# A gated linear-attention recurrence on one Trainium2 core: small products as tiles of TensorE, and a new order of the pieces

## The chip, the cores and the metric

One core of one Trainium2 chip runs the whole program. The metric is the device time of one execution in microseconds (us); less is better. TensorE (PE) multiplies, VectorE (DVE), ScalarE (ACT) and GpSimd (POOL) do elementwise work, SyncE (SP) issues most transfers. Before the change the median of 3 runs is 4453.52 us (4452.66 to 4456.73).

## The reference, cut to what matters

The program computes two layers over 16 x 1024 tokens of 256 features: a normalization, a recurrent attention block, a mixture of 8 experts (expert choice), a second recurrence (a linear state-space scan) and a gated feed-forward block. The change touches the recurrent attention block alone:

```python
delta = shifted - h
x_lerp = h + delta * x_proj_mu
x0 = jnp.tanh(x_lerp @ xl_w1.T) @ xl_w2.T + xl_b2          # 256 -> 32 -> 160
x1 = jnp.tanh(x0).reshape(B_, T_, 5, R)                    # 5 groups of 32
x2 = jnp.einsum('btnr,hnr->btnh', x1, x_out_w.reshape(H_, 5, R))
mus = x2 + x_bias
r_mu, w_mu, k_mu, v_mu, g_mu = (mus[:, :, i] for i in range(5))
r = (h + delta * r_mu) @ r_w.T
w_in = h + delta * w_mu
w = jnp.tanh(w_in @ w_w1.T) @ w_w2.T + w_b                 # 256 -> 64 -> 128
k = (h + delta * k_mu) @ k_w.T
v = (h + delta * v_mu) @ v_w.T
g = (h + delta * g_mu) @ g_w.T
wd = jnp.exp(-jnp.exp(w.reshape(B_, T_, NH, DK)))
...
o_t = jnp.einsum('bhk,bhkv->bhv', r_t, S) + jnp.sum(r_t * bonus * k_t, -1, keepdims=True) * v_t
S = S * w_t[..., None] + k_t[..., None] * v_t[..., None, :]
...
o = (o * gn_weight + gn_bias) * jax.nn.silu(g)
return o @ o_w.T
```

There are 4 heads of 32 keys and 64 values. All of it is fp32.

## The kernel before, in words

The function `recurrence_phase` cuts the 1024 tokens of each of the 16 sequences into chunks of 128. A **group** is 4 sequences times one chunk of 128 tokens, so 512 tokens (`GN`); there are 32 groups (`GROUPS`), in order. Tiles hold features on the 128 partitions and the 512 tokens along the free dimension.

Three sorts of work are interleaved, in an order written out by hand in `sequence`, which every engine walks through:

- `piece(f, ...)`: the projections of group f, from the mixed input to receptance, keys, decay, values and gates. Each product has a number `n`, `bank(n)` says in which PSUM bank it lands, `emptied` waits until ACT or DVE has read an earlier product. The products by name: LOW (256 -> 32, tile a_low), X0 and X0T (32 -> 128 and 32 -> 32, tiles a_x1 and a_x1t), ten mixing products MIX (a_xo and, for the fifth mixture, a_xot; two for each of five mixtures), DLOW (256 -> 64) and DEXP (64 -> 128) for the decay, KEY, REC, OWN (the token's own product r*bonus*k, summed by heads, 4 columns at a time), two of VAL and two of GATES. After a mixing product DVE forms a_tmp (L1164), then POOL a_mix (L1077).
- `level(g, lv)`: seven levels that build the 128 x 128 lower triangle A of products inside a chunk. In each, PE multiplies keys by receptance for 4 sequences x 4 heads as row tiles of 32 (L1467) into the four banks `ps_heads` (banks 0 to 3, the level banks); then DVE scales keys, receptance and decay (L1190, L1192, L1194) and, in levels 0 to 4, copies the products under a mask into a_A (L1203); in levels 5 and 6 ACT copies them (L1322). PE begins the next level when both are done. At level 0 the copy also waits until ACT has written the diagonal of A: 16 activations (L1299, tile a_A) that follow ACT's copy of OWN (L1295, a_own).
- `chunk(g, u)`: transposed keys (L1481), the outputs o from the state and from A (L1501, L1504; two halves), the update U of the state (L1493), the normalization (reduction L1231, `pow` on POOL L1091, scaling L1236), transposes (L1516), gating (L1241) and the output product with a_ow.

Before the change all pieces use banks 6 and 7 in turn, and all but the levels and U are products on the whole array; where the weight has only 32 or 64 rows it is padded with zero rows to 128. While group g goes through its levels, the pieces of group g+1 and the rest of the chunk of g-1 fill the spaces. POOL's `ahead` computes a_delta for group g+2, and DVE's `begin` computes a_lerp (L1148) for it. A matmul in fp32 appears in the profile as two instructions (two passes).

Of the kernel before, what the change touches and what calls it, by code (L numbers as in the profile page):

```python
# [735 lines left out]
def recurrence_phase(nc, ctx, ps, ps_heads, xnT_d, s0_d, acc_d, left_d, ident, score, idxT, gateT, idxL, gateL, w):  # L736

    with ExitStack() as mem:
# [11 lines left out]
        w2 = sb("a_w2", [P, NMU * RANK])  # L750
        b2 = sb("a_b2", [P, 1])
        b2t = sb("a_b2t", [RANK, 1])
        xo = sb("a_xo", [P, NMU - 1, D])
        xot = sb("a_xot", [P, D])
# [6 lines left out]
        dw2 = sb("a_dw2", [P, KW])  # L761
# [10 lines left out]
        low = sb("a_low", [P, GN])  # L772
        x1 = sb("a_x1", [P, GN])
        x1t = sb("a_x1t", [P, GN])
        tmp = [sb(f"a_tmp{r}", [P, GN]) for r in range(2)]
        mix = [sb(f"a_mix{n}", [P, KD, GN]) for n in range(NMU)]
        dlow = sb("a_dlow", [P, GN])
# [91 lines left out]
        LOADS = 21  # L869
        PADDED = 7  # L870
        SET = PADDED + 8
        READY = SET + NH + 2
        order = [1, 2, 0, 3, 4]
        SLOTS = 9
        CHUNK = LEVELS
        LATE = 2
        FRONT = SLOTS - LATE + 1
        MIX = [3, 4, 5, 6, 8, 9, 13, 14, 16, 17]
        LOW, X0, X0T, DLOW, DEXP, KEY, REC, OWN, VAL, GATES = 0, 1, 2, 7, 10, 11, 12, 15, 18, 20
        USES = 22  # L880
        BY_ACT = [LOW, X0, X0T, DLOW, DEXP, KEY, REC, OWN, VAL, VAL + 1]
        BY_DVE = MIX + [GATES, GATES + 1]
        AT = {2: (0, 1), 3: (2, 3), 4: (4, 5), 6: (6, 7), 7: (8, 9)}
# [6 lines left out]
        def later(j, q, n):  # L890

            return (j + (q + n) // QB, (q + n) % QB)

        def emptied(eng, f, n):

            if n < 0:
                f, n = f - 1, n + USES
            if n in BY_ACT:
                eng.wait_ge(act_out, len(BY_ACT) * f + BY_ACT.index(n) + 1)
            else:  # L900
                eng.wait_ge(dve_out, len(BY_DVE) * f + BY_DVE.index(n) + 1)

        def bank(n):
            return ps[6 + n % 2]

        def sequence(eng, ahead, begin, piece, level, chunk, extra=None):

            def group(j, q, first, left):
                g = QB * j + q
                f1, f2 = later(j, q, 1), later(j, q, 2)  # L910
                r = q % 2

                def chunk_at(s):
                    if s >= CHUNK:
                        chunk(g, j, q, s - CHUNK, first)
                    elif not first:
                        jp, qp = later(j - 1, q, QB - 1)
                        chunk(g - 1, jp, qp, s + SLOTS - CHUNK, isinstance(j, int) and j == 0 and q == 1)

                def piece_at(s):  # L920
                    if s < LATE:
                        piece(g, q, FRONT + s, first)
                    elif left:
                        piece(g + 1, f1[1], s - LATE if s < CHUNK else s - LATE + 1, False)

                for s in range(SLOTS):
                    if s < LEVELS:
                        level(g, r, s, first)
                    if left and s == CHUNK:
                        piece(g + 1, f1[1], CHUNK - LATE, False)  # L930
                    if extra and s == CHUNK:
                        extra(g, s)
                    if s < LATE or s == SLOTS - 1:
                        piece_at(s)
                        chunk_at(s)
                    else:
                        chunk_at(s)
                        piece_at(s)
                        if extra and s < CHUNK:
                            extra(g, s)  # L940
                    if left > 1 and s == CHUNK:
                        ahead(g + 2, f2[0], f2[1])
                    if left > 1 and s == SLOTS - 1:
                        begin(g + 2, f2[1], False)

            ahead(0, 0, 0)
            begin(0, 0, True)
            for s in range(FRONT):
                piece(0, 0, s, True)
            ahead(1, 0, 1)  # L950
            begin(1, 1, False)
            for q in range(QB):
                group(0, q, q == 0, 9)
            for j in range(1, NE - 1):
                for q in range(QB):
                    group(j, q, False, 9)
            for q in range(QB):
                group(NE - 1, q, False, QB - 1 - q)
            for u in range(SLOTS - CHUNK, SLOTS):
                chunk(GROUPS - 1, NE - 1, QB - 1, u, False)  # L960
# [4 lines left out]
        def _(sp):  # L965
            loads = [(mu[:], w["L0_attn_x_proj_mu"]), (w1[:], w["L0_attn_xl_w1"]),
                     (b2[:], w["L0_attn_xl_b2"][0:P]), (b2t[:], w["L0_attn_xl_b2"][P:P + RANK]),
# [5 lines left out]
            for dst, src in loads:  # L973
                sp.dma_start(dst, src).then_inc(w_in, 16)
            padded = [(w2[0:RANK, :], w["L0_attn_xl_w2"]), (dw2[0:GATE, :], w["L0_attn_w_w2"]),
                      (xot[0:RANK, :], w["L0_attn_x_out_w"][P:P + RANK])]
# [5 lines left out]
            assert len(loads) + len(padded) == LOADS + 1  # L982

            def load(j, q, first):
                for k in range(KD):
                    if first:
                        sp.dma_start(h[q % 2][:, k, :, 1:P + 1], hT_v[k, :, GT * q:GT * (q + 1), 0:P]
                                     ).then_inc(h_in[q % 2], 16)
                    else:
                        sp.dma_start(h[q % 2][:, k], hT_v[k, :, GT * q:GT * (q + 1), bass.ds(P * j - 1, P + 1)]  # L990
                                     ).then_inc(h_in[q % 2], 16)

            def store(j, q):
                sp.wait_ge(s0_sb, 2 * (QB * j + q) + 2)
                sp.sem_inc(spare, 1)
                sp.dma_start(s0_v[bass.ds(j, 1), :, GT * q:GT * (q + 1), :].rearrange("o p b d -> (o p) b d"),
                             s0[q % 2][:]).then_inc(s0_out[q % 2], 16)

            def group(j, q, first):

                f2 = later(j, q, 2)
                sp.wait_ge(mixed, NMM * (QB * j + q + 1))
                sp.sem_inc(spare, 1)
                load(f2[0], f2[1], first and q < 2)
                if not first or q:
                    store(*((j, q - 1) if q else (j - 1, QB - 1)))

            load(0, 0, True)
            load(0, 1, True)
            for q in range(QB):  # L1010
                group(0, q, True)
            for j in range(1, NE - 1):
                for q in range(QB):
                    group(j, q, False)
            for q in range(QB):
                if q < 2:
                    group(NE - 1, q, False)
                else:
                    store(NE - 1, q - 1)
# [7 lines left out]
            store(NE - 1, QB - 1)  # L1027
# [5 lines left out]
        def _(pool):  # L1033
            nc.gpsimd.memset(zeros[:], 0.0).then_inc(zeroed, 1)
            for operand in (xo, w2, xot, dw2, low, x1t, dlow):
                nc.gpsimd.memset(operand[:], 0.0).then_inc(set_up, 1)
# [15 lines left out]
            pool.wait_ge(w_in, 16 * (LOADS + 1))  # L1052
# [13 lines left out]
            def begin(f, q, first):  # L1066
                pass
# [13 lines left out]
            def level(g, r, lv, first):  # L1081
                pass
# [1205 lines left out]
```

## Time and profile before

| | us |
|---|---|
| median of 3 runs | 4453.52 |
| the profiled execution, its own time | 4459.22 |
| its span | 4456.3 |
| the recurrence, from its first to its last product (213.2 to 1759.8) | 1547 |
| one group of it, in the middle (716.63 to 763.85) | 47.22 |

Over the span PE is busy 93%, DVE 62%, ACT 43%, POOL 38%. A row of the timeline gives the start and the length of a run of like instructions, engine, line, what it writes and reads, shapes and count, and in brackets the idle time before it with the one that ended it. Matmuls are pipelined: the length of the last one reaches past the point at which the next may begin, so the time that a product takes is the difference of the starts of two rows. A row on a stretch gives its bounds and length, then the busy time (and instructions) of PE, PE's weight loads, DVE, ACT and POOL, PE's granted clock (1.00 is 2.4 GHz, 0.50 is 1.2 GHz), the share of the DMA engines and GB/s.

### The profile page before, as it was taken

How to read it: one execution, taken by the hardware profiler on the slowest of the kernel's cores; microseconds unless marked ns; L12 is line 12 of the kernel's file. 1: busy time of each engine (PE TensorE's matmuls, PEld its weight loads, DVE VectorE, ACT ScalarE, POOL GpSimd, SP SyncE). 2: the span in 40 equal slices, each digit the busy share in tenths (PEclk: the TensorE clock that was granted, in tenths of full speed). 3: DMA queues.
4: the chain of work that ended last, by engine and by line, in shares of the span. 5: the costliest groups of instructions: out<-in, count | busy, mean ns of one | idle time of the engine just before them, and what ended most of it. 6: DMA issues, size and time to landing. Idle time of an engine off the chain costs nothing. (4 is left out here: it accounts for less than half of the span.)

```text
span 4456.3 us, 72817 instructions
## 1 busy us (share of the span) xinstructions
PE 4138.4 (93%) x28636; PEld 3280.3 (74%) x28636; DVE 2755.8 (62%) x5175; ACT 1931.6 (43%) x3576; POOL 1690.0 (38%) x1337
## 2 busy tenths in 40 slices
PE   8699999999999997999999999999995999999894
PEld 8556566566565564889888888989894777788774
DVE  6467777777777775443434344343433788888886
ACT  2134444444444443544444454444442444444441
POOL 2233333333333342443444344344432233433333
PEclk9999999999999998999999999999997999999998
DMA  9501111111110101232323233232224343444423
GB/s 313 162 25 35 34 34 34 34 35 34 39 34 30 39 30 64 56 61 41 67 44 64 39 70 59 44 66 46 41 34 127 96 101 79 112 110 96 112 56 43
DMA packets 254003, 294.21 MB, mean 66 GB/s; under 512 B 21600, under 2 KB 226656, under 8 KB 251616
## 3 DMA queue, kind: packets, MB, share of 16 engines
q0 software_dynamic: 88064, 117.74, 15.8%
q1 hardware_dynamic: 165600, 171.82, 12.0%
q8 instruction: 228, 3.74, 0.3%
q14 instruction: 111, 0.91, 0.1%
HBM read 155.15 MB, written 134.35 MB: 65 GB/s over the span
## 5 line engine op out<-in xcount | busy, mean ns | idle before, releaser
L564 DVE TENSOR_TENSOR e_hTl<-e_hf,e_hTh 128x512 fp32r<-128x512 f32 x512 | 354.6, 693 | 801.6 <-ACT e_hTh L506 762.5
L1077 POOL TENSOR_TENSOR a_mix<-a_tmp,a_h 128x512 f32<-128x512 f32 x320 | 389.4, 1237 | 797.7 <-PE ps L1376 745.5
L425 POOL DMA_INDIRECT acc_d<-e_y,e_sids x256 | 408.6, 1596 | 708.9 <-DVE e_y L580 656.1
L505 ACT ACTIVATE e_hf<-ps_heads,e_b 128x512 f32<-128x512 f32 x512 | 354.2, 692 | 679.7 <-PE ps_heads L663 621.3
L663 PE MATMUL ps<-e_w2h,e_hTh 128*128 128x256 f32 x2048 | 578.7, 283 | 0.0
L663 PE MATMUL ps<-e_w2h,e_hTl 128*128 128x256 f32 x2048 | 577.3, 282 | 0.3 <-issue 0.2
L663 PE MATMUL ps<-e_w2l,e_hTh 128*128 128x256 f32 x2048 | 571.6, 279 | 0.8 <-issue 0.6
L663 PE MATMUL ps_heads<-e_xTh,e_w1h 128*128 128x512 f32 x1024 | 418.7, 409 | 16.2 <-ACT e_hTh L506 10.3
L663 PE MATMUL ps_heads<-e_xTl,e_w1h 128*128 128x512 f32 x1024 | 405.6, 396 | 0.0
L663 PE MATMUL ps_heads<-e_xTh,e_w1l 128*128 128x512 f32 x1024 | 405.6, 396 | 0.0
L663 PEld LDWEIGHTS ps<-e_w2h,e_hTh 128*128 128x128 f32 x2048 | 385.7, 188 | 20.3
L663 PEld LDWEIGHTS ps<-e_w2h,e_hTl 128*128 128x128 f32 x2048 | 385.6, 188 | 18.3
L663 PEld LDWEIGHTS ps<-e_w2l,e_hTh 128*128 128x128 f32 x2048 | 387.2, 189 | 1.1 <-issue 1.1
L1467 PEld LDWEIGHTS ps_heads<-a_R,a_K 32*128 32x128 f32 x7168 | 224.5, 187 | 178.0 <-issue 175.9
L506 ACT ACTIVATE e_hTh<-ps_heads,e_b 128x512 fp32r<-128x512 f32 x512 | 349.8, 683 | 0.0
L1164 DVE SCALAR_TENSOR_TENSOR a_tmp<-ps,a_xb,a_delta 128x512 f32<-128x512 f32 x320 | 240.1, 751 | 162.3 <-PE ps L1376 138.2
L402 POOL DMA_INDIRECT e_x<-xn_d,e_gids x256 | 255.6, 998 | 174.1 <-PE ps_heads L647 97.5
L1467 PE MATMUL ps_heads<-a_R,a_K 32*128 32x64 f32 x7168 | 252.7, 277 | 35.7 <-DVE a_A L1203 35.6
L1203 DVE COPY_PREDICATED a_A<-a_mask,ps_heads 128x1024 f32<-128x1024 uint32 x160 | 275.2, 1720 | 0.0
L1376 PE MATMUL ps<-a_x,a_xo 128*128 128x512 f32 x512 | 246.3, 603 | 0.7 <-ACT a_R L1290 0.7
L663 PEld LDWEIGHTS ps_heads<-e_xTh,e_w1h 128*128 128x128 f32 x1024 | 194.0, 189 | 56.9 <-ACT e_hTh L506 24.2
L2058 ACT CAST f_hTh<-ps 128x512 fp32r<-128x512 f32 x160 | 93.8, 586 | 311.5 <-DVE ps L1878 311.5
(293 smaller groups left out, 9390.8 us busy)
## 6 DMA issues: line engine op xcount, KB each, us to landing
r_x<-in_L_attn_hidden_states SPq DMA_DIRECT2D x32, 512.0 KB, 6.4
xn_d<-r_xn SPq DMA_DIRECT2D x32, 512.0 KB, 4.6
xnT_d<-r_xT SPq DMA_DIRECT2D x32, 512.0 KB, 3.9
acc_d<-a_zeros POOLq DMA_DIRECT2D x32, 512.0 KB, 3.0
s_d<-a_s SPq DMA_DIRECT2D x32, 512.0 KB, 2.8
e_w<-in_L_ffn_w SPq DMA_DIRECT2D x16, 1024.0 KB
f_a<-acc_d SPq DMA_DIRECT2D x32, 512.0 KB, 3.8
f_x<-s_d SPq DMA_DIRECT2D x32, 512.0 KB, 5.2
```

The costliest lines, as they stand in the source:

```text
L402: pool.indirect_dma_start(xg[r][:, t, :], None, xn_d, bass.IndirectOffsetOnAxis(ap=gids[:, GT * q + t:GT * q + t + 1], axis=0)).then_inc(x ...
L425: pool.indirect_dma_start(acc_d, bass.IndirectOffsetOnAxis(ap=sids[:, GT * q + t:GT * q + t + 1], axis=0), ys[r][:, t, :], None, compute_o ...
L505: nc.scalar.activation(hf[m % 2][:], ps[2 + m % 2][:], ACT.Gelu, bias=b1s[:, m:m + 1])
L506: nc.scalar.activation(hT[q % 2][0][:, m, :], ps[2 + m % 2][:], ACT.Gelu, bias=b1s[:, m:m + 1]).then_inc(hi_sb, 1)
L564: nc.vector.tensor_tensor(hT[q % 2][1][:, m, :], hf[m % 2][:], hT[q % 2][0][:, m, :].bitcast(F32), ALU.subtract).then_inc(h_sb, 1)
L663: last = nc.tensor.matmul(out, lhsT, rhs, start=(first and n == 0), stop=(end and n == len(pairs) - 1))
L1077: nc.gpsimd.tensor_tensor(mix[n][:, m, :].rearrange("p (c t) -> p c t", c=GT), tmp[i % 2][:].rearrange("p (c t) -> p c t", c=GT), h[q % 2] ...
L1164: stt(out=tmp[i % 2][:], in0=bank(MIX[i])[:], scalar=xb[:, n, m:m + 1], in1=delta[r][:, m].rearrange("p c t -> p (c t)"), op0=ALU.add, op1 ...
L1203: nc.vector.copy_predicated(a4, m4.unsqueeze(1).to_broadcast([P, NH * GT, nb, half]), pairs_ps(half)).then_inc(A_sb, 1)
L1376: done = nc.tensor.matmul(to, lhsT, rhs, start=(k == 0), stop=(k == len(pairs) - 1))
L1467: done = nc.tensor.matmul(ps_heads[:, hd, c * P:c * P + P // 2].rearrange("p (n t) -> p n t", t=half), K2[r][rows, tok], R2[r][rows, tok]. ...
L2058: nc.scalar.copy(hT[0][:, m, :], ps[4 + m % 2][:]).then_inc(hh_sb, 1)
```

## The change

Five things are changed in `recurrence_phase`; nothing outside it.

1. **Mixing products as row tiles.** Of the first four mixtures, the weights of two sit on rows 0 to 63 and of the other two on rows 64 to 127. `side_by_side` issues two mixing products, one on each half of the rows (64 x 128 weights, 512 columns), into two banks. The fifth mixture (`last_mix`) is also cut in two row tiles of 64, each with two products of 256 columns.
2. **Small projections as column tiles by tokens.** LOW becomes 4 column tiles of 32, one for each 128 tokens; DLOW two column tiles of 64, one for each 256 tokens; X0T four column tiles of 32 over 128 tokens, twice. Their results now fill all partitions with fewer columns, so a_low is 128 x 128, a_x1t and a_dlow 128 x 256, and the activations on them are shorter. X0 becomes four products of 128 columns, DEXP two of 256, with weights padded by zeros (a_w2, a_dw2, a_xot gain copies in other rows).
3. **Banks.** DLOW, KEY, two mixing products, REC and OWN land in the level banks 0 to 3 (six uses), after the levels of the group before are done (a wait on A_sb).
4. **Order.** `sequence` is written out anew for one group, with 15 pieces and 9 units of the chunk; the pieces 0 to 11 of group g+1 stand between level 2 of group g and level 0 of g+1, the value and gate products (12 to 14) between its first levels. Of the old order, the values and gates were there too; the second half of o and U stood before level 0; now only U does, and the second half of o stands after level 1 of the next group. OWN (piece 11) is now the last piece before U and level 0.
5. **Setup.** 10 more small loads of weights (32 in all instead of 22), three memsets less.

```diff
-        order = [1, 2, 0, 3, 4]
-        MIX = [3, 4, 5, 6, 8, 9, 13, 14, 16, 17]
-        LOW, X0, X0T, DLOW, DEXP, KEY, REC, OWN, VAL, GATES = 0, 1, 2, 7, 10, 11, 12, 15, 18, 20
-        AT = {2: (0, 1), 3: (2, 3), 4: (4, 5), 6: (6, 7), 7: (8, 9)}
+        PIECES, LATE = 15, 12
+        UNITS = 9
+        LOW, X0, X0T, DLOW, KEY, DEXP, REC, OWN, VAL, GATES = 0, 1, 2, 9, 10, 13, 14, 17, 18, 20
+        MIX = [3, 4, 5, 6, 7, 8, 11, 12, 15, 16]
+        MIXED = [(1, 0), (2, 0), (1, 1), (2, 1), (0, 0), (3, 0), (0, 1), (3, 1), (4, 0), (4, 1)]
+        BANKS = [6, 7, 6, 7, 6, 7, 6, 7, 6, 0, 1, 2, 3, 7, 0, 7, 6, 1, 6, 7, 6, 7]
+        AT = {2: (0, 1), 3: (2, 3), 4: (4, 5), 7: (6, 7), 10: (8, 9)}
...
         def bank(n):
-            return ps[6 + n % 2]
+            return ps[BANKS[n]]
...
+            for g in range(GROUPS):
+                level(g, 0)
+                piece(g, 12)
+                level(g, 1)
+                preceding(g - 1, 2)
+                piece(g, 13)
+                level(g, 2)
+                preceding(g - 1, 3)
+                piece(g, 14)
+                following(g + 1, 0)
+                level(g, 3)
+                preceding(g - 1, 4)
+                following(g + 1, 1)
+                level(g, 4)
+                preceding(g - 1, 5)
+                following(g + 1, 2)
+                level(g, 5)
+                preceding(g - 1, 6)
+                following(g + 1, 3)
+                step(g, 5)
+                level(g, 6)
+                preceding(g - 1, 7)
+                following(g + 1, 4, 5)
+                step(g, 6)
+                preceding(g - 1, 8)
+                following(g + 1, 6)
+                step(g, 7)
+                chunk(g, 0)
+                following(g + 1, 7)
+                if g + 2 < GROUPS:
+                    ahead(g + 2)
+                following(g + 1, 8, 9, 10, 11)
+                chunk(g, 1)
+                if g + 2 < GROUPS:
+                    begin(g + 2)
...
 (TensorE)
+                def room(n):
+                    used = [m for m in range(n) if BANKS[m] == BANKS[n]]
+                    if used:
+                        emptied(pe, f, used[-1])
+                    elif f and BANKS[n] < NH:
+
+                        pe.wait_ge(A_sb, LEVELS * f)
+                    elif f:
+                        emptied(pe, f - 1, max(m for m in range(USES) if BANKS[m] == BANKS[n]))
+                    return bank(n)
+
+                def side_by_side(i):
+
+                    to = [room(MIX[i]), room(MIX[i + 1])]
+                    rows = [slice(0, P // 2), slice(P // 2, P)]
+                    if i == 0:
+                        emptied(pe, f, X0)
+                    for v in range(2):
+                        n, m = MIXED[i + v]
+                        nc.tensor.matmul(to[v][:], xo[rows[v], n, m * P:(m + 1) * P], x1[rows[v], :], start=True, stop=True
+                                         ).then_inc(piece_ps, 1)
+
+                def last_mix(i):
+
+                    to = [room(MIX[i]), room(MIX[i + 1])]
+                    emptied(pe, f, X0T)
+                    for u in range(2):
+                        for v in range(2):
+                            rows = slice(P // 2 * v, P // 2 * (v + 1))
+                            done = nc.tensor.matmul(to[v][:, HALF * u:HALF * (u + 1)], xot[rows, u, v * P:(v + 1) * P],
+                                                    x1t[rows, :], start=True, stop=True)
+                            if u:
+                                done.then_inc(piece_ps, 1)
                 if s == 0:
+                    to = room(LOW)
                     pe.wait_ge(lerped, 2 * f + 2)
-                    product(room(LOW)[0:RANK, :], [(w1[:, k, :], lerp[:, k, :]) for k in range(KD)]).then_inc(piece_ps, 1)
+                    for k in range(KD):
+                        for c in range(GT):
+                            done = nc.tensor.matmul(to[RANK * c:RANK * (c + 1), 0:P], w1[:, k, :],
+                                                    lerp[:, k, c * P:(c + 1) * P], start=k == 0, stop=k == KD - 1)
+                    done.then_inc(piece_ps, 1)
                 if s == 1:
                     to = room(X0)
                     emptied(pe, f, LOW)
-                    product(to[:], [(w2[:, 0:P], low[:])]).then_inc(piece_ps, 1)
+                    for c in range(GT):
+                        done = nc.tensor.matmul(to[:, c * P:(c + 1) * P], w2[:, c, 0:P], low[:], start=True, stop=True)
+                    done.then_inc(piece_ps, 1)
                     to = room(X0T)
-                    product(to[0:RANK, :], [(w2[:, P:P + RANK], low[:])]).then_inc(piece_ps, 1)
+                    for n in range(2):
+                        for c in range(GT):
+                            done = nc.tensor.matmul(to[RANK * c:RANK * (c + 1), n * P:(n + 1) * P],
+                                                    w2[:, c % 2 * 2 + n, P:P + RANK], low[:], start=True, stop=True)
+                    done.then_inc(piece_ps, 1)
+                if s in (2, 3, 4, 7):
+                    side_by_side(AT[s][0])
                 if s == 5:
+                    to = room(DLOW)
+                    have_mix(1)
+                    for k in range(KD):
+                        for u in range(2):
+                            done = nc.tensor.matmul(to[GATE * u:GATE * (u + 1), 0:HALF], dw1[:, k, :],
+                                                    mix[1][:, k, HALF * u:HALF * (u + 1)], start=k == 0, stop=k == KD - 1)
+                    done.then_inc(piece_ps, 1)
+                if s == 8:
+                    to = room(DEXP)
+                    emptied(pe, f, DLOW)
+                    for u in range(2):
+                        done = nc.tensor.matmul(to[:, HALF * u:HALF * (u + 1)], dw2[:, u, :], dlow[:], start=True, stop=True)
+                    done.then_inc(piece_ps, 1)
```

The pieces on PE by number are: 0 LOW, 1 X0 and X0T, 2, 3 and 4 pairs of mixing products, 5 DLOW, 6 KEY, 7 a pair, 8 DEXP, 9 REC, 10 the last mixture, 11 OWN, 12 VAL, 13 and 14 GATES. The units of the chunk are: 0 transposed keys and the first half of o, 1 U, 2 the second half of o (on DVE the state), 3 the variance, 4 the scaling, 5 and 6 transposes (6 and 7 on DVE the gating), 7 and 8 the output product. `step` is DVE's share of the routing (L1113, L1118, L1124), as before.

## Rows read from the trace of the kernel before

**Rows 1.** Busy time by engine over a stretch of 31 groups.
```profile
240.00:1708.00 1468.00, 1435.02 (x12310) 884.16 (x12303) 1112.29 (x1701) 668.15 (x1454) 541.68 (x404) 1.00 0.10 34
```
**Rows 2.** Timeline of PE over one group (start, length, line, what).
```profile
705.93 0.60 PE L1501 MATMUL ps<-a_Sd,a_R 128*128 128x256 f32 x2
...
708.52 1.94 PE L1376 MATMUL ps<-a_x,a_xo 128*128 128x512 f32 x4
710.45 1.05 PE L1423 MATMUL ps<-a_heads,a_rk 128*128 128x4 f32 x8
711.36 1.96 PE L1376 MATMUL ps<-a_x1t,a_xot 128*128 128x512 f32 x4
...
713.25 0.65 PE L1493 MATMUL ps<-a_V,a_KT 128*32 128x64 f32 x32
...
716.63 1.12 PE L1467 MATMUL ps_heads<-a_R,a_K 32*128 32x64 f32 x32
717.68 3.72 PE L1376 MATMUL ps<-a_vw,a_mix 128*128 128x256 f32 x16
721.63 1.12 PE L1467 MATMUL ps_heads<-a_R,a_K 32*128 32x64 f32 x32 [0.23 <-DVE a_A L1203]
722.68 3.70 PE L1376 MATMUL ps<-a_mix,a_gw 128*128 128x512 f32 x8
726.34 1.12 PE L1467 MATMUL ps_heads<-a_R,a_K 32*128 32x64 f32 x32
```
**Rows 3.** Timelines of ACT, DVE and POOL over the same group.
```profile
711.59 0.17 ACT L1295 COPY a_own<-ps 128x16 f32<-128x16 f32 x1 [1.78 <-PE ps L1423]
711.80 4.78 ACT L1299 ACTIVATE a_A<-ident,a_own 128x128 f32<-128x128 f32 x16
...
712.50 1.61 DVE L1164 SCALAR_TENSOR_TENSOR a_tmp<-ps,a_xb,a_delta 128x512 f32<-128x512 f32 x2 [1.25 <-PE ps L1376]
...
719.04 2.43 DVE L1203 COPY_PREDICATED a_A<-a_mask,ps_heads 128x1024 f32<-128x1024 uint32 x1
721.28 1.18 DVE L1231 TENSOR_REDUCE a_vare<-a_sq 128x16 f32<-128x1024 f32 x1
...
722.87 0.44 DVE L1190 TENSOR_TENSOR a_K<-a_K,a_decays 128x256 f32<-128x256 f32 x1 [0.20 <-PE ps_heads L1467]
...
729.14 1.23 DVE L1203 COPY_PREDICATED a_A<-a_mask,ps_heads 128x1024 f32<-128x1024 uint32 x1
...
739.94 1.42 DVE L1190 TENSOR_TENSOR a_K<-a_K,a_decays 128x256 f32<-128x256 f32 x1 [0.40 <-PE ps_heads L1467]
...
722.75 2.93 POOL L1091 TENSOR_TENSOR a_rstd<-a_vare,a_power 128x16 f32<-128x16 f32 x1 [5.19 <-DVE a_vare L1232]
...
748.34 2.31 POOL L1077 TENSOR_TENSOR a_mix<-a_tmp,a_h 128x512 f32<-128x512 f32 x2 [2.57 <-PE ps L1376]
```
**Rows 4.** Timeline of PE in the last group.
```profile
1722.29 1.12 PE L1467 MATMUL ps_heads<-a_R,a_K 32*128 32x64 f32 x32 [2.47 <-DVE a_A L1203]
1723.34 1.09 PE L1516 MATMUL ps<-ident,a_oc 128*128 128x128 f32 x4
1725.68 1.99 PE L1467 MATMUL ps_heads<-a_R,a_K 32*128 32x64 f32 x32 [1.25 <-DVE a_A L1203]
```
**Rows 5.** Stretches with PE's granted clock (the number before the DMA share).
```profile
1723.50:1730.00 6.50, 5.25 (x42) 4.31 (x42) 4.80 (x10) 1.02 (x2) 0.00 (x0) 0.50 0.00 0
...
3634.90:3638.20 3.30, 3.30 (x18) 3.30 (x16) 3.20 (x7) 1.17 (x2) 1.39 (x2) 0.50 0.23 14
...
4172.30:4175.70 3.40, 3.33 (x28) 3.13 (x29) 3.30 (x11) 1.40 (x3) 1.63 (x2) 1.00 1.09 366
```
**Rows 6.** PE's waits of that length in the second layer, the first, tenth and last of 12.
```profile
3634.37 1.54 PE L2110 MATMUL ps_heads<-ident,f_xn 128*128 128x128 f32 x8 [2.16 <-ACT f_xn L2017]
...
4172.23 1.09 PE L2110 MATMUL ps_heads<-ident,f_xn 128*128 128x128 f32 x8 [2.31 <-ACT f_xn L2017]
...
4296.66 1.64 PE L2110 MATMUL ps_heads<-ident,f_xn 128*128 128x128 f32 x8 [2.00 <-ACT f_xn L2017]
```

More of the change, by code:

```diff
@@ L903, in bank @@
         def bank(n):
-            return ps[6 + n % 2]
+            return ps[BANKS[n]]
         def sequence(eng, ahead, begin, piece, level, chunk, extra=None):
[L908 to L960, printed above, removed]
+            def following(f, *pieces):
+                if f < GROUPS:
+                    for s in pieces:
+                        piece(f, s)
@@ new lines, in preceding, with step @@
+            def preceding(g, u):
+                if g >= 0:
+                    chunk(g, u)
+            def step(g, s):
+                if extra:
+                    extra(g, s)
+            for f in range(2):
+                ahead(f)
+                begin(f)
+                if f == 0:
+                    following(0, *range(LATE))
+            for g in range(GROUPS):
[33 more added lines that the diff above has]
+                    begin(g + 2)
@@ L962, in recurrence_phase @@
+            for u in range(2, UNITS):
+                chunk(GROUPS - 1, u)
         block = mem.enter_context(nc.Block())
@@ L993, in store @@
[L993 to L1019, printed above, removed]
+                    to, first = h[q % 2][:, k], P * j - 1
+                    if j == 0:
+                        to, first = h[q % 2][:, k, :, 1:P + 1], 0
@@ L1064, in ahead, with begin, piece @@
                                         ).then_inc(deltas, 1)
-            def begin(f, q, first):
+            def begin(f):
                 pass
-            def piece(f, q, s, first):
+            def piece(f, s):
                 for i in AT.get(s, ()):
-                    n, m = order[i // KD], i % KD
+                    n, m = MIXED[i]
                     emptied(pool, f, MIX[i])
-                    if not first:
-                        last_use = (DLOW, KEY, REC, VAL + 1, GATES + 1)[i // KD]
+                    if f:
+                        last_use = (REC, DLOW, KEY, VAL + 1, GATES + 1)[n]
                         pool.wait_ge(piece_ps, USES * (f - 1) + last_use + 1)
@@ L1459, in level @@
                 else:
-                    emptied(pe, g, REC)
-                if not first or lv:
+                    emptied(pe, g, OWN)
+                    emptied(pe, g, MIX[7])
+                if n:
                     pe.wait_ge(A_sb, n)
```

308 lines of the change are left out of this document (147 added, 161 removed).

## The prediction

> **What bounds the kernel now.** I read first the busy time over a stretch of 31 groups, then the timeline of each engine over one group, then the end of the recurrence and the clock in several stretches. In the steady part PE is busy 1435 of 1468 us, DVE 1112, ACT 668 and POOL 542, at the full clock throughout [rows 1]. A group lasts 47.2 us, so PE is busy 46.2, DVE 35.8 and ACT 21.5 us of it. The timeline of PE shows hardly a gap: from level 0 at 716.63 to level 1 at 721.63 it computes VAL and then waits 0.23 [rows 2]. So each product removed from PE can shorten the group, until something else is late. What could be late is the chain through the levels: level, DVE's scaling, masked copy, next level. Level 1 starts at 721.63, DVE follows at 722.87, 1.24 later; the masked copy takes 2.43 us in levels 0 and 1 and 1.23 from level 2 on [rows 2, 3].
>
> **What the change takes off PE.** A pass of 512 columns on the whole array takes 0.43 us: eight of them (GATES) take 3.66 with the entry [rows 2]. Per group:
> - Four pairs of mixing products: 16 passes become 8 if the two row tiles overlap, -3.43. That they do is shown by the levels: 32 passes of 64 columns, which one after another would need 32 x 0.054 = 1.71, take 1.05 [rows 2]. U, column tiles, takes 0.65 for as many [rows 2].
> - Last mixture: 4 passes to 2, -0.86. LOW: 4 passes to a quarter, -1.29. X0T: 2 passes to half, -0.43. DLOW: 4 to half, -0.86. X0 and DEXP keep their columns, 0.
> - Sum: -6.9. But each change between tiling modes costs about 0.1 us, on the way in and out: the level that follows VAL or GATES gives 3.66 for 3.43 of passes. I count 26 changes of mode in a group after, 19 before: +0.7, with bounds 0 and 7 x 0.2 = 1.4.
>
> So PE's work falls from 46.2 to about 40; at face value 6.2 x 31 = -190 us. DVE's 35.8 us of work are still below that. The rest of this section asks whether the new order lets PE have it.
>
> The Trainium skill says the same of the modes: TensorEngine Tiling, section Key Properties, states that changing the tiling mode drains TensorE. It agrees with the rows and gives no price. A price against the change is in TensorE: Matmul & The Clock Gate, section Measured speedup vs the span model: four row tiles gave 3.07x, not 4x. By that efficiency a pair would take 0.86 / 0.77 = 1.12 instead of 0.86 us. No row of before has tiles of 64 rows. By it, three pairs on the stretch from level 6 to OWN below would add 0.8 us a group.
>
> **The new group, step by step.** I walk through one group with these durations, from one event that is late to the next. Latencies from rows: DVE 1.24 after the start of a level, PE 0.1 after a copy's end, others about 0.2.
>
> 1. *OWN to level 1: 8.75.* OWN takes 0.91 (710.45 to 711.36), ACT's copy starts 1.14 after OWN's start, the 16 activations of the diagonal 1.35 after it and last 4.78 [rows 2, 3]. In the old order 6.2 us lay between OWN and level 0 (710.45 to 716.63); in the new one only U does, so level 0 starts 1.6 after OWN. DVE's copy of level 0 needs the diagonal, done at 6.2 after OWN; then 2.43 and 0.1. (The lerp, DVE's work ahead of level 0, ends earlier.) On PE in that time: level 0 (1.05) and VAL (3.6, as many columns as GATES), done at 6.25. **PE then waits 2.5 us.** This is the wait that replaces the old one of 0.23.
> 2. *Level 1 to 2: 5.55.* PE: level 1.05, second half of o 0.1 + 2.59 (705.93 to 708.52), one gate 1.8 [rows 2]. DVE needs 1.24 + 0.9 + 2.43 + 0.1 = 4.7, hidden.
> 3. *Level 2 to 3: 3.55.* DVE first needs the tanh of the gate that has just ended (1.4), then scaling 0.8, copy 1.23, 0.1. PE: 1.05 + 1.8 + LOW 0.55, hidden.
> 4. *Level 3 to 4: 3.9.* DVE: variance 1.36, gate 0.6, scaling 0.8, copy 1.23, less what overlaps the level. X0 waits 0.8 for the bank that this gate empties.
> 5. *Level 4 to 5: 3.6.* POOL's `pow` takes 2.93 after the variance [rows 3]; then DVE's scaling of o, 1.2, then the level's own 2.1. PE waits 0.6 before the transposes.
> 6. *Level 5 to 6: 3.2.* Two a_tmp (1.53) stand ahead of the scaling, which collides with POOL's a_mix; such a scaling took 1.42 instead of 0.44 [rows 3].
> 7. *Level 6 to OWN: 17.85*, PE's own: level 1.05, output product 1.83, pair 1.17 (0.86, entry, load, drain), DLOW 1.0, output 1.85, KEY 1.72 (four passes), transposed keys 0.44, o 2.53, pair 1.1, DEXP 0.96, REC 1.72, last mixture 1.2, and one wait of 1.3: REC needs the a_mix of the pair two steps ahead, that is 0.2 + a_tmp 0.8 + 1.16 [rows 3] against DEXP alone.
>
> Sum: 8.75 + 5.55 + 3.55 + 3.9 + 3.6 + 3.2 + 17.85 = **46.4 us**, only 0.8 under 47.2. PE would idle some 7 us in it. I give this sum 0.7 either way.
>
> **What the wait of 2.5 us does to the clock.** The trace has such waits. In the last group, where the pieces have run out, PE waits 2.47 us for the masked copy before a level; after it the four transposes take 1.09 instead of 0.66, the next level 1.99 instead of 1.12 [rows 4], and the clock is 0.50 (1.2 GHz) over 6.5 us [rows 5]. In the second layer there are 12 waits of 2.0 to 2.4 us, all for ACT's f_xn (three shown [rows 6]); after 7 the clock was 0.50 for some 3.3 us, after 5 it stayed at 1.00 (one of each shown [rows 5]). Around those waits PE is dense; around the new one stand a level, then the narrow products of o, as in the last group. The new wait (2.5 us by this sum) comes in every group, and what follows it (step 2) is PE's own time. A stretch of 6.8 us at half clock there takes 3.4 us more, one of 3.4 us takes 1.7. Bounds a group: 7 of 12 times 1.7 = +1.0; 3.4 + 1.7 = +5.1, if the thin stretch from level 3 to 5 drops the clock as well. I take +3.4, since the last group is nearest in kind.
>
> So a group lasts 46.4 + 3.4 = 49.8, +2.6 on 47.2, and 31 groups give +80 us. Filling and end I take as equal: the first pieces run alone in both, the last group is bound by the level chain in both. The ten small loads go before DVE's masks are made, hidden. The profiled execution took 4459.22 us (span 4456.3), so 4539 for it; that one lay 5.7 over the median of 4453.52, so the forecast is **4533 us**, 1.8% slower.
>
> **Rivals.**
> - *A: the clock holds, the new order gains little* (0.20). 46.4 a group: -0.8 x 31 = -25, 4428 us. For it: 5 of the 12 waits. Against it: the last group. By the clock page of the skill, section Why this matters for your kernels, only idle gaps of over about 3 us are to be avoided; by that alone these waits of 2.5 cost no clock and this case would stand. The wait of 2.47 in the last group disagrees. It decides for faster once fewer than about a quarter of the groups lose 3.4 us (0.8 / 3.4).
> - *B: short drops only* (0.12). 46.4 + 1.0 = 47.4: +5, 4459 us.
> - *C: the change does all that it says* (0.03). PE stays dense at 41: -190, 4263 us. Against it stands step 1, where ACT's 4.78 and DVE's 2.43 are in series.
> - *D: two drops a group* (0.20 of the slow case). 46.4 + 5.1 = 51.5: +133, 4587 us.
> - *E: the row tiles of 64 do not overlap* (0.05). Three pairs on step 7 cost 0.86 each, 49.0 without the clock: +56, 4510 us.
>
> **How the numbers follow.** The forecast with D holds 0.60, A 0.20, B 0.12, C 0.03, E 0.05. Faster by over 0.2% (9 us, about what the measurement can tell from no change): A, C and a little of B, 0.24. Same: the middle of B, 0.07. Slower: the rest, 0.69. The range goes from A (4428, less a little for its 0.7 either way) to D (4587): 4424 to 4590. Below it lie C and the better half of A, above it the worst of D. The likeliest case alone has 4490 to 4590.
>
> **What would show it.** In the profile after: the granted clock of the recurrence at 0.85 to 0.95 instead of 1.00; PE waiting some 2.4 us on DVE's a_A before level 1 of each group, and that copy starting right behind ACT's 16 activations; pairs of mixing products in about 0.9 us; REC behind a POOL a_mix; PE busy share down from 98%. Wrong would make it: a clock of 1.00 (then A), pairs of 1.7 us (E), a level 1 that starts 5 us after level 0 (C).

## The result and the profile after

The changed kernel takes **4536.45 us** (median of 4 runs, 4533.74 to 4545.7) where the kernel before took 4455.12 on the same chip (4452.66 to 4464.64): ratio 1.0182, 95% interval 1.0161 to 1.0203. The forecast was 4533.

The profile of after: span 4532.0 us, PE busy 89% where it was 93%. First the page: the busy line, PE's granted clock in 40 slices, and two of the costliest groups (their idle time stands behind the bar, with what ended it).

```profile
PE 4045.5 (89%) x29980; PEld 3332.8 (74%) x29980; DVE 2762.2 (61%) x5175; ACT 1904.9 (42%) x3576; POOL 1690.8 (37%) x1334
...
PEclk9999999999999898899999999999997999999998
...
L1486 PE MATMUL ps_heads<-a_R,a_K 32*128 32x64 f32 x7168 | 268.5, 288 | 130.7 <-DVE a_A L1183 106.7
...
L1183 DVE COPY_PREDICATED a_A<-a_mask,ps_heads 128x1024 f32<-128x1024 uint32 x160 | 275.8, 1724 | 31.9 <-ACT a_A L1280 31.9
```

PE waits 130.7 us ahead of its levels, mostly for DVE's masked copy; that copy itself is idle 31.9 us, about 1.0 a group, for ACT's diagonal. A row of stretches, where rows 1 had 1435.02 us of PE in 1468 and a clock of 1.00, then two shorter ones:

```profile
240.00:1700.00 1460.00, 1272.21 (x12959) 883.15 (x12958) 1067.26 (x1619) 607.05 (x1372) 509.46 (x379) 0.94 0.10 33
736.20:746.20 10.00, 9.94 (x136) 7.06 (x137) 7.57 (x12) 4.04 (x9) 0.00 (x0) 1.00 0.01 2
...
783.30:793.50 10.20, 10.17 (x56) 7.75 (x56) 3.98 (x6) 1.08 (x2) 0.00 (x0) 0.50 0.01 2
```

The second and third lie at the same place of two neighbouring groups, from level 1 on. In one the clock is 1.00, in the next it is 0.50 (1.2 GHz) for 10.2 us. Below, a group that holds such a low stretch is called dropped, one without it undropped. PE's timeline shows one of each, from the value products on, the dropped one to level 2 (beside rows 2):

```profile
728.98 1.12 PE L1486 MATMUL ps_heads<-a_R,a_K 32*128 32x64 f32 x32
730.03 3.72 PE L1357 MATMUL ps<-a_vw,a_mix 128*128 128x256 f32 x16
...
776.05 1.12 PE L1486 MATMUL ps_heads<-a_R,a_K 32*128 32x64 f32 x32
777.10 3.72 PE L1357 MATMUL ps<-a_vw,a_mix 128*128 128x256 f32 x16
783.33 1.98 PE L1486 MATMUL ps_heads<-a_R,a_K 32*128 32x64 f32 x32 [2.50 <-DVE a_A L1183]
785.24 1.22 PE L1521 MATMUL ps<-a_Sd,a_R 128*128 128x256 f32 x2
786.25 1.81 PE L1524 MATMUL ps<-a_V,a_A 128*128 128x64 f32 x8
...
790.41 3.46 PE L1357 MATMUL ps<-a_mix,a_gw 128*128 128x512 f32 x4
793.80 1.12 PE L1486 MATMUL ps_heads<-a_R,a_K 32*128 32x64 f32 x32
```

Level 0 to level 1 is 7.28 us, with a wait of 2.50; rows 2 had 5.00 and 0.23. The same 32 instructions of a level take 1.98 in the low stretch and 1.12 outside it, and level 1 to level 2 takes 10.47 us where it takes 5.62 in the undropped group. From 728.98 to 776.05 a group lasts 47.07 us, the next, from 776.05 to 827.96, 51.91. They alternate like this through nearly the whole recurrence: 16 of the 32 groups hold a low stretch of 10.2 us (15 of the groups 1 to 30), and groups 0 and 26 one of 6.8.

What stands ahead of level 1, on ACT and DVE (beside rows 3):

```profile
728.56 0.17 ACT L1276 COPY a_own<-ps_heads 128x16 f32<-128x16 f32 x1 [0.68 <-PE ps_heads L1455]
728.76 4.79 ACT L1280 ACTIVATE a_A<-ident,a_own 128x128 f32<-128x128 f32 x16
```
```profile
728.88 2.82 DVE L1131 SCALAR_TENSOR_TENSOR a_lerp<-a_delta,a_mu,a_h 128x512 f32<-128x512 f32 x2
...
732.30 0.41 DVE L1174 TENSOR_TENSOR a_decays<-a_decay 128x256 f32<-128x256 f32 x1
733.69 2.42 DVE L1183 COPY_PREDICATED a_A<-a_mask,ps_heads 128x1024 f32<-128x1024 uint32 x1 [0.98 <-ACT a_A L1280]
```

The reader is to see two queues that end near each other: ACT's diagonal at 733.5, DVE's own work at 732.7. The copy starts behind the later, and PE's level 1 (736.26) behind the copy.

**Where the 75.7 us between the two spans are.** The first level 0 comes 3.0 us earlier (236.73 after, 239.69 before). Group 0 is 7.6 shorter (44.47, 52.03). The 30 groups after it last 49.60 in the mean where they lasted 47.23: +71.3. The last group, to the recurrence's last product, takes 65.0 instead of 51.3: +13.7. All that follows: +1.2.

### The profile page after: what moved, and what is told of

The parts are those of the page before. It is cut to its first block and busy times, and to the rows that moved or that the text cites. A ratio compares the mean times of both kernels' runs of the same rounds, so it can differ in the third digit from the quotient of the medians.

```text
span 4532.0 us, 75480 instructions
## 1 busy us (share of the span) xinstructions
PE 4045.5 (89%) x29980; PEld 3332.8 (74%) x29980; DVE 2762.2 (61%) x5175; ACT 1904.9 (42%) x3576; POOL 1690.8 (37%) x1334
## 5 line engine op out<-in xcount | busy, mean ns | idle before, releaser
L1486 PEld LDWEIGHTS ps_heads<-a_R,a_K 32*128 32x128 f32 x7168 | 240.0, 198 | 244.3 <-issue 191.4
L1486 PE MATMUL ps_heads<-a_R,a_K 32*128 32x64 f32 x7168 | 268.5, 288 | 130.7 <-DVE a_A L1183 106.7
L1074 POOL TENSOR_TENSOR a_rstd<-a_vare,a_power 128x16 f32<-128x16 f32 x32 | 93.7, 2928 | 587.8 <-DVE a_vare L1212 587.8
L1183 DVE COPY_PREDICATED a_A<-a_mask,ps_heads 128x1024 f32<-128x1024 uint32 x160 | 275.8, 1724 | 31.9 <-ACT a_A L1280 31.9
L663 PEld LDWEIGHTS ps_heads<-e_xTl,e_w1h 128*128 128x128 f32 x1024 | 193.6, 189 | 46.5
```

Of the source, the lines that this page charges most:

```text
L663: last = nc.tensor.matmul(out, lhsT, rhs, start=(first and n == 0), stop=(end and n == len(pairs) - 1))
L1074: nc.gpsimd.tensor_tensor(rstd[:], vare[:], power[:], ALU.pow).then_inc(rstd_sb, 1)
L1183: nc.vector.copy_predicated(a4, m4.unsqueeze(1).to_broadcast([P, NH * GT, nb, half]), pairs_ps(half)).then_inc(A_sb, 1)
L1486: done = nc.tensor.matmul(ps_heads[:, hd, c * P:c * P + P // 2].rearrange("p (n t) -> p n t", t=half), K2[r][rows, tok], R2[r][rows, tok]. ...
```

## The experiments

All ratios below are to the kernel before on the same chip, which there took 4436 to 4443 us (4455 on the first). The windows quoted cover 1170 us of the recurrence.

### filler: only the wait is filled

```diff
+                if lv == 1 and g:
+                    pe.wait_ge(sq_sb, 2 * g - 1)
+                    for _ in range(2):
+                        nc.tensor.matmul(ps[5][:], ident[:], x1[:], start=True, stop=True)
```

> The changed kernel with two extra products of 128 x 512 (1.7 us, results thrown away) on PE between VAL and level 1, inside the wait of 2.5 us; no dependency is changed. Theory (the clock): PE's wait falls to about 0.8 us, the granted clock stays at 1.00 from the second group on, every group takes the 47.1 us that the undropped ones take now, so 15 or 16 groups lose 4.85 us each: about 4461 us, as fast as before the change within 10 us. Rival (the time was lost to waits and drains of the new order itself, and the low clock is only its sign): 4536 us or more, since work was only added.

Measured: 4431.01 us, ratio 0.9988 (0.9978 to 0.9998). The stretch, then PE ahead of level 1 (the kernel's lines from 1476 on are 4 later than in after):

```profile
330.00:1500.00 1170.00, 1057.60 (x11016) 722.92 (x11016) 902.97 (x1371) 517.44 (x1167) 432.46 (x322) 1.00 0.11 35
```
```profile
756.98 1.88 PE L1478 MATMUL ps<-a_x,ident 128*128 128x512 f32 x4
759.67 1.12 PE L1490 MATMUL ps_heads<-a_R,a_K 32*128 32x64 f32 x32 [0.81 <-DVE a_A L1183]
760.72 0.70 PE L1525 MATMUL ps<-a_Sd,a_R 128*128 128x256 f32 x2
...
763.42 1.94 PE L1357 MATMUL ps<-a_mix,a_gw 128*128 128x512 f32 x4
765.28 1.12 PE L1490 MATMUL ps_heads<-a_R,a_K 32*128 32x64 f32 x32
```

Products that nobody reads give back 1.9% (1.0182 against 0.9988), some 86 us: level 1 starts as late as in after, but no group from 1 to 30 holds a low stretch, and a group lasts 47.06. So the whole loss against the kernel before is the clock, and without it the change is worth nearly nothing. Every later size of a part is taken against this run where the clock has to be out of the way.

### o_early and o_split: other work into the wait

o_early moves the second half of o ahead of level 1; o_split moves only half of that half (one of its two blocks of 128 tokens, as a unit of its own, number 9).

```diff
                 piece(g, 12)
-                level(g, 1)
                 preceding(g - 1, 2)
+                level(g, 1)
```

> The changed kernel with the second half of o (2.6 us of PE) moved from behind level 1 to ahead of it. PE then has 1.05 + 3.6 + 2.6 between level 0 and level 1 for the same 7.28 us, but only 1.05 + 1.9 between levels 1 and 2, where DVE's chain of 4.7 decides: the wait moves there and is 1.8 us instead of 2.5. Both theories: step 2 falls from 5.6 to 4.7, a group from 47.1 to 46.2. Clock theory: 4430 us if a wait of 1.8 between a product of the gates and a level does not lower the clock, up to 4530 if it does, with the low stretch now behind level 2. Rival without the clock: 4510 us (4536 less 0.9 x 31).

Measured: 4417.52 us, ratio 0.9961 (0.9946 to 0.9975). Undropped groups take 46.06. In 18 of the groups 1 to 30 a low stretch of 3.4 us follows the wait that has moved to level 2, and such a group takes 47.0 to 47.1 (one 47.45):

```profile
762.11 1.12 PE L1486 MATMUL ps_heads<-a_R,a_K 32*128 32x64 f32 x32 [1.66 <-DVE a_A L1183]
763.16 3.10 PE L1357 MATMUL ps<-a_mix,a_gw 128*128 128x512 f32 x4
766.19 1.08 PE L1410 MATMUL ps<-a_lerp,a_w 128*32 128x128 f32 x16
```

The dense gate product (1.92 in an undropped group of that run, 3.03 here) falls into it, so the dense product that followed this wait did not keep the clock.

> The changed kernel with the second half of o cut in two: one sequence's part (1.3 us) ahead of level 1, one behind it. The same work and the same sum of waits as in the run before (1.9 us), but as 1.2 us ahead of level 1 and 0.6 ahead of level 2. Clock theory: no wait is long enough, clock 1.00, a group 46.2 us, 4427 us. Rival without the clock: as the run before, 4510 us.

Measured: 4436.68 us, ratio 1.0004 (0.9994 to 1.0013), clock 0.97. The undropped group is 46.07 as expected, but the clock of 1.00 that I expected did not come: 20 of the groups 1 to 30 have a low stretch, 14 of 3.4 us (47.4 a group) and 6 of 6.8 (48.9). The wait ahead of level 1 is only 1.25:

```profile
718.32 1.12 PE L1487 MATMUL ps_heads<-a_R,a_K 32*128 32x64 f32 x32 [1.25 <-DVE a_A L1184]
719.37 0.70 PE L1522 MATMUL ps<-a_Sd,a_R 128*128 128x256 f32 x2
719.90 1.50 PE L1525 MATMUL ps<-a_V,a_A 128*128 128x64 f32 x8
```

So a wait of 1.25 us with narrow products on both sides can lower the clock as well, while in the filler run 0.81 with the same products behind it did not.

### pair_early: the wait for REC

```diff
-                chunk(g, 0)
                 following(g + 1, 7)
+                chunk(g, 0)
```

> The changed kernel with the pair of mixing products for REC (piece 7) moved ahead of the transposed keys and the first half of o, so that POOL's a_mix is done when REC comes. Expected: PE's wait of 1.17 us before REC is gone, an undropped group takes 45.9 us. The wait of 2.5 before level 1 stays, and with it the clock: with every second group dropped, 4500 us; which groups drop may change with the length of the group, so 4425 (none) to 4575 (all). Rival: the a_tmp of the moved pair delays DVE's other work and nothing is won, 4536 us.

Measured: 4511.98 us, ratio 1.0169 (1.0152 to 1.0186). REC's wait is gone and level 6 to the next level 0 takes 18.2 us instead of 19.6. But now every group has a low stretch, of 6.8 or 10.2 us but for two of 3.4, and the clock is 0.91:

```profile
330.00:1500.00 1170.00, 1050.35 (x10288) 734.14 (x10284) 848.10 (x1286) 487.78 (x1105) 406.65 (x301) 0.91 0.10 33
```

The 1.4 us of each group went back to the clock: the two ratios, 1.0169 and 1.0182, do not differ.

### half_diagonal: what sets the wait

```diff
-                    for hd in range(NH):
+                    for hd in range(NH // 2):
```

> The changed kernel with only heads 0 and 1 of ScalarE's diagonal written (the other 8 of the 16 activations are left out, so half of the diagonal of A is not filled). Theory: in the changed kernel VectorE's masked copy starts when the last of ScalarE's 16 activations (4.79 us) ends, after an idle of 1.0 us; with 8 of them (2.4 us) it starts when VectorE's own two lerp operations and the three decay operations end, 1.0 us earlier. So level 0 to level 1 takes 6.3 us instead of 7.28, the wait ahead of level 1 is 1.5 us instead of 2.5, and an undropped group is 46.1 instead of 47.07. A wait of 1.5 us can still lower the clock in part of the groups (0.97 to 0.98 granted): 4425 to 4470 us on a chip where the kernel before is 4436 (ratio 0.998 to 1.008). Rival 1, ScalarE's diagonal does not set the wait: 7.28 and 2.5 remain, 4517 us. Rival 2, the diagonal sets all of the wait: level 0 to level 1 shrinks by the whole 2.4 us to 4.9, no wait, clock 1.00, 4360 us.

Measured: 4457.43 us, ratio 1.0029 (1.0016 to 1.0042). Level 0 to level 1 takes 6.22 us, the wait is 1.45, and DVE's copy follows its own work without idle time:

```profile
710.52 1.12 PE L1486 MATMUL ps_heads<-a_R,a_K 32*128 32x64 f32 x32 [1.45 <-DVE a_A L1183]
```
```profile
707.61 0.42 DVE L1174 TENSOR_TENSOR a_decays<-a_decay 128x256 f32<-128x256 f32 x1
707.95 2.42 DVE L1183 COPY_PREDICATED a_A<-a_mask,ps_heads 128x1024 f32<-128x1024 uint32 x1
```

The diagonal sets 1.0 us of the wait; below that DVE's lerp and decays are late next, 1.45 more. In the profiled execution 12 of the groups 1 to 30 still drop, for 6.8 us: 49.3 against 46.0. That execution took 4438 us, the least of seven; the others took 4447 to 4460, so the number of dropped groups is probably larger in them.

### whole_filled and small_long: the two parts of the saving, priced at the full clock

whole_filled is filler with the four pairs of mixing products over all 128 rows. The weight's other rows hold zeros, so the sums stay the same; my expectation said otherwise and was wrong in that.

```diff
-    nc.tensor.matmul(to[v][:], xo[rows[v], n, m * P:(m + 1) * P], x1[rows[v], :], ...
+    nc.tensor.matmul(to[v][:], xo[:, n, m * P:(m + 1) * P], x1[:], ...
```

> The run filler (clock held at 1.00, groups of 47.06) with the four pairs of mixing products of a group as two products over all 128 rows each instead of two row tiles of 64 side by side (each of these eight products then adds both mixtures, so the values differ from the reference). Theory: two row tiles stream side by side, a pair is 1.06 us; whole, it is 2 x 0.86 = 1.72 us, +0.66. The pairs after levels 4 and 5 lie ahead of waits of 0.6 and 0.7 us and are mostly absorbed; the pairs of the stretch after level 6 are not: +1.3 to +1.5 us a group, 48.4 to 48.6, ratio 1.009 to 1.011 over the filler run, some 1.008 to 1.010 over before (4473 us where before is 4436). Rival, the row tiles do not overlap (my rival E): no difference from the filler run, 4431 us. Second rival, the absorbed pairs cost in full too: +2.6 us a group, 4513 us.

Measured: 4503.18 us, ratio 1.0142 (1.0125 to 1.0159); groups of 49.02, clock 1.00 but for one group (25), where the wait ahead of level 1 was 1.15 instead of 0.80 and a low stretch of 6.8 us followed (52.6 us). A pair, its start to the next start, after and here:

```profile
712.36 1.13 PE L1390 MATMUL ps<-a_x,a_xo 64*128 64x512 f32 x4
713.42 1.08 PE L1432 MATMUL ps_heads<-a_mix,a_dw 128*64 128x256 f32 x8
```
```profile
705.37 1.88 PE L1390 MATMUL ps<-a_x,a_xo 128*128 128x512 f32 x4
707.18 1.08 PE L1432 MATMUL ps_heads<-a_mix,a_dw 128*64 128x256 f32 x8
```

1.06 us side by side, 1.81 whole: the row tiles overlap, and the pair itself is 0.75 shorter. The output product ahead of it takes 0.10 longer when tiles follow (1.93 in filler, 1.83 here, start to start), so a pair saves some 0.65, as expected. Of the four, the two after level 6 cost 1.34 together and the ones after levels 4 and 5 cost 0.28 and 0.33, since the waits there (0.31, 0.75) take up only a part. So the four pairs, part 1 without the last mixture, are worth 1.96 us a group. The expected 48.4 to 48.6 was too low, since these last two pairs still cost 0.6 together.

small_long is filler with LOW issued three times over, X0T and DLOW twice.

```diff
-                    for k in range(KD):
+                    for k in 3 * list(range(KD)):
```

> The run filler (clock 1.00, groups of 47.06) with the small projections made as long as they were on the whole array, the tiles kept: LOW's 16 instructions three times over (0.57 us becomes 1.7), X0T's and DLOW's twice (0.58 becomes 1.1, 1.0 becomes 2.0); the results are the same. It prices the second part of the change (column tiles by tokens), 2.7 us of PE's work. Theory: DLOW lies on PE's own stretch after level 6 and costs all of its 1.0; LOW lies ahead of level 3, where PE hardly waits, and costs 1.1; X0T lies ahead of a wait of 0.3 and costs 0.3, and the wait of 0.7 ahead of X0 shrinks, since level 3 is later. Sum +1.8 to +2.4 a group, 48.9 to 49.5, ratio to before 1.011 to 1.016 (where the filler run had 0.9988). Rival: the waits between levels 2 and 6 take up all but DLOW, +1.0 a group, ratio 1.006.

Measured: 4470.1 us, ratio 1.008 (1.0063 to 1.0096); groups of 48.12, clock 1.00. This is the rival's size, +1.06, not the +1.8 to +2.4 of my theory. DLOW costs 0.86, as level 6 to level 0 shows (20.46 against 19.60). In one of the groups 1 to 30 (25, as in whole_filled) the clock dropped here as well, for 6.8 us behind a wait of 1.14 ahead of level 1. filler and pair_filled have the same wait once, in the same group, and no drop. LOW adds 0.86 ahead of level 3, and the steps from level 3 to 6 give back 0.66, since DVE and POOL, which PE waits for there, work on in that time. Part 2, as far as this prices it (some 2.2 us more of PE), is worth half of what it takes off PE.

### pair_filled, two_moves and all_three: the moves together

pair_filled is pair_early with filler's two products; two_moves is o_early and pair_early together; all_three is two_moves and one 128 x 512 product in the wait ahead of level 2.

> The run pair_early (the pair of mixing products of piece 7 ahead of the chunk's transposes, REC's wait gone) with the two products of the run filler in the wait ahead of level 1. Theory: what pair_early gained in the walk (level 6 to level 0 in 18.2 instead of 19.6 us) it lost to a low clock in every group; with the wait filled the clock stays at 1.00 and the gain shows: groups of 45.7 us, 43 us less than the filler run, 4388 us where before is 4436 (ratio 0.989). Rival: the low stretches come from elsewhere in the new order (the thin work between levels 3 and 6), then groups stay at 47 to 49 us and the time at 4430 to 4510.

Measured: 4397.06 us, ratio 0.9902 (0.9886 to 0.9919), groups of 45.67, clock 1.00. pair_early's gain was real and the clock had hidden it.

> The changed kernel with the three moves together: the output products of the group before ahead of level 1 (o_early), piece 7's pair ahead of the chunk's transposes (pair_early), and one 128x512 product that nobody reads in the wait of 1.65 us that o_early left ahead of level 2. Theory: undropped groups of o_early are 46.06; less 1.4 for the pair is 44.66; the filled wait leaves 0.8 us, as in the filler run where the clock held, so the clock is 1.00 and the time 4431 - 31 x 2.4 = 4357 us where before is 4436 (ratio 0.982). Rival 1: the waits of 0.6 to 0.8 us that are left at levels 2 to 6 are enough to lower the clock for 3.4 us in two groups of three (+1 us each, as in o_early): 4378. Rival 2: the gains of the two moves overlap (the second only shifts the wait for POOL's mixture): 4390 or more.

(What this text calls the output products is the second half of o, which o_early moves.)

Measured: 4366.29 us, ratio 0.9831 (0.9814 to 0.9847), groups of 44.68, clock 1.00:

```profile
735.87 1.02 PE L1478 MATMUL ps<-a_x,ident 128*128 128x512 f32 x2
737.70 1.12 PE L1490 MATMUL ps_heads<-a_R,a_K 32*128 32x64 f32 x32 [0.81 <-DVE a_A L1183]
```

> The run all_three without its added product: o_early and pair_early together, nothing in the wait of 1.65 us ahead of level 2. It tells what the added product is worth there. Theory: that wait lowers the clock for 3.4 us in some two groups of three, as in o_early, and each of these takes 1.0 us more: 45.3 a group in the mean, 4387 us where before is 4443 and all_three was 4366 (ratio 0.987). Rival 1: shorter groups all drop, as they did in pair_early, and for 6.8 us: +2 to +3 us each, 4430 us or more. Rival 2: the product is worth nothing, the clock stays at 1.00: 4363 us.

Measured: 4366.07 us, ratio 0.9844 (0.9828 to 0.9861). Only 6 of the groups 1 to 30 hold a low stretch, each of 3.4 us (45.7 a group against 44.67), with the same wait of 1.65 behind which 18 dropped in o_early:

```profile
330.00:1500.00 1170.00, 1064.58 (x11517) 744.04 (x11517) 944.98 (x1434) 544.64 (x1232) 460.33 (x340) 0.99 0.11 37
...
701.61 1.12 PE L1486 MATMUL ps_heads<-a_R,a_K 32*128 32x64 f32 x32 [1.65 <-DVE a_A L1183]
```

I had expected two in three. The added product is worth nothing that these times can tell, since the two intervals overlap; the traces give it 0.2 us a group (44.69 in the mean with it, 44.88 without). two_moves has no idle work in it and beats both kernels: 1.6% faster than before and, by the two ratios, 3.3% faster than after (0.9844 / 1.0182 = 0.967). It is the version to take.

## Why the prediction was right

**The mechanism.** The step on which the sign hung was the wait of 2.5 us ahead of level 1 and the clock behind it. Both came: 2.51 and 2.50 in the two groups shown, and in the second of them a clock of 0.50 behind it. That this clock is the cause is shown by filler, which changes nothing else and takes the loss away. Without it rival A would have stood, if smaller: it gave -25 us to a clock that holds, and filler's ratio of 0.9988 is -5. The Trainium skill, TensorE: Matmul & The Clock Gate, section Why this matters for your kernels, asks only to avoid idle gaps above about 3 us; the waits of 2.5, 1.66, 1.45 and 1.25 in these runs, each with a clock of 0.50 behind it in 12 or more of the groups 1 to 30, disagree.

**The walk, step by step**, in undropped groups:

| step | predicted | measured |
|---|---|---|
| OWN to level 1 | 8.75 | 8.85 |
| level 1 to 2 | 5.55 | 5.62 |
| level 2 to 3 | 3.55 | 3.56 |
| level 3 to 4 | 3.9 | 3.84 |
| level 4 to 5 | 3.6 | 3.65 |
| level 5 to 6 | 3.2 | 3.52 |
| level 6 to OWN | 17.85 | 18.03 |
| sum | 46.4 | 47.07 |

The sum lies at the edge of the 0.7 that I gave it. Half of the difference is level 5 to 6, where both scalings of DVE collide with POOL's a_mix and not one of them:

```profile
752.71 1.41 DVE L1147 SCALAR_TENSOR_TENSOR a_tmp<-ps,a_xb,a_delta 128x512 f32<-128x512 f32 x2
754.17 0.82 DVE L1170 TENSOR_TENSOR a_K<-a_K,a_decays 128x256 f32<-128x256 f32 x1
754.92 1.39 DVE L1172 TENSOR_TENSOR a_R<-a_R,a_decays 128x256 f32<-128x256 f32 x1
```
```profile
753.54 2.49 POOL L1061 TENSOR_TENSOR a_mix<-a_tmp,a_h 128x512 f32<-128x512 f32 x2 [3.94 <-DVE a_tmp L1147]
```

This matters for the verdict on the change itself: at a held clock it gives not 0.8 a group but 0.16, and that is the 0.9988 of filler.

**The clock's term.** I took 3.4 us in each group, as one stretch of 6.8. It is 4.85 in every second group, as one stretch of 10.2: 2.5 in the mean (49.60 less 47.07). So this term was too large by 0.9 and the walk too small by 0.7, and the mean group, 49.60, came within 0.2 of the forecast 49.8 by two errors that cancel. That closeness, and with it that of 4533 to 4536, is luck; the direction and the mechanism are not. The bounds (1.0 to 5.1) held both.

**Filling and end.** I took them as equal. The first group is 7.6 us shorter and the beginning 3.0, the last group 13.7 longer. Of these 7.5 lie ahead of its level 6: its level 1 waits 2.5 and its clock drops, and the second half of o of the group before, which had stood ahead of its level 0, now stands inside it. The other 6.2 lie behind level 6, where the output product of the group before now stands (1803.94 to 1810.11); before the change it stood ahead of level 6. In filler, where its clock holds at level 1, the last group takes 59.5 us instead of 65.0, so 5.5 of the 13.7 are the clock. Beginning and end together are +3.1; this error is small only because the parts cancel.

**The rivals.** E fell: a pair takes 1.06, not 1.8. My own estimate of a pair in step 7 (1.17 and 1.1) was near: measured are 1.06, or 1.16 with the 0.10 on the product ahead (the 0.9 among the signs was too low). The estimate of 1.12 worked out from the 3.07x for four row tiles in the Trainium skill, TensorE: Matmul & The Clock Gate, section Measured speedup vs the span model, lies nearer to the measured 1.06 than the 0.86 of perfect overlap. B and D name the ends of what a group can lose; single groups of o_split lie at B's end (+1.35), those of after at nearly D's (+4.85). C was out of reach: even the best order found takes 44.7 a group, not 41, with 4.1 of the 6.2 us of waits still there.

**Where the saving went.** PE's work fell nearly as forecast: the waits listed in an undropped group add up to 6.2 us, so 40.8 of work are left of 46.2 (about 40 was forecast). By the two experiments at full clock, undoing the four pairs of part 1 costs 1.96 and part 2 some 1.06. If these add up (not tried together), the new order with the old products would take 50.1 us, 2.9 more than the old order's 47.2; neither run undoes the tiles of the last mixture, so it may be more. So the new order would spend nearly all that the tiles are worth in it, 3.0, and the clock then takes 2.5 more. That this sum holds is worked out, not shown, and the opposite test, the new tiles in the old order, was not run.

**What stays open.** Which groups drop. It is every second one in after, all in pair_early, 18 in o_early and 6 in two_moves with the same wait as in o_early. The length of the wait alone does not say it. The traces point to the moment at which a group comes. In o_early all groups from 1 to 30 are alike up to level 2, dropped or not (but for 0.35 us in group 25), and the low stretches start between 12.60 and 14.06 us after level 0 of their group. From one dropped group to the next the start slides by 0.7: 12.93 and 13.63, then an undropped group; 12.65, 13.36 and 14.06, then an undropped one. The six of two_moves start between 12.62 and 13.87. So the length of a whole group, which sets when the next one comes, may decide how often a given wait costs the clock. In after a dropped and an undropped group together last 98.98 us nearly throughout, and the pattern repeats with them. This is read from the starts and argued, not shown: no run shifts the groups in time and changes nothing else.

## What to carry to other kernels

Work taken off the bounding engine pays in full only where that engine does not wait (undoing part 2 put some 2.2 us on PE and cost 1.06): before counting the saving, walk one period from one late event to the next and find the chain (here ACT's diagonal, DVE's masked copy, level 1) that the removed work had covered. When TensorE gains a wait of over a microsecond in each period, look at the granted clock behind it before anything else, and test it with a product that nobody reads; here one such run told that the loss was all clock. Then fill the wait with real work from behind it (the second half of o) and judge small moves only at a held clock, since pair_early's 1.4 us a group looked worthless until then.

## What the hardware showed that was not expected

The low clock came behind waits as short as 1.25 us (o_split, 20 of the groups 1 to 30) and 1.15 (whole_filled and small_long, once each; filler and pair_filled had that wait once without it), not only behind 2.5; behind 0.81 (filler, pair_filled, all_three) none of these groups had it. In these groups its stretches lasted 3.4, 6.8 or 10.2 us, and in after they came in every second group with the same wait of 2.5 in both kinds. Two fp32 products on row tiles of 64 took 1.06 us for a pair where the same pair on the whole array took 1.81, a factor of 1.7; with the 0.10 that the product ahead of the tiles took longer it is 1.6.
